# Query and key transposes of the windowed attention put into the score banks 0 and 1 instead of bank 2

## The reference

```python
x = x + _L0_attn_a_ref(_layernorm(x), ...)   # linear attention, 16 heads of 16
x = x + _L0_ffn_ref(_layernorm(x), ...)      # 256 -> 1024 -> 256, ternary weights, relu
x = x + _L0_attn_b_ref(_layernorm(x), ...)   # attention in a window of 64, 16 heads, 4 key heads
x = x + _L0_ffn_ref(_layernorm(x), ...)      # the same feed-forward weights again
```

```python
scores = jnp.einsum('bhqd,bhkd->bhqk', q, k_full) * scale
scores = jnp.where(mask[None, None], scores, jnp.finfo(scores.dtype).min)
att = jax.nn.softmax(scores, axis=-1)
y = jnp.einsum('bhqk,bhkd->bhqd', att, v_full)
...
out = y.transpose(0, 2, 1, 3).reshape(bsz, seqlen, dim) @ Wo.T
```

## Time and profile before

| | before |
|---|---|
| median of 3 runs | 3016.64 us (3013.68 to 3021.11) |
| the profiled execution's own time | 3018.86 us |
| its span | 3017.0 us |
| PE busy | 2801.0 us, 93% |
| DVE busy | 2297.0 us, 76% |
| ACT busy | 1746.8 us, 58% |
| POOL busy | 500.9 us, 17% |
| mean granted clock of TensorE | 0.977 of full speed |

### The profile page before, as it was taken

One profiled execution on the slowest core, in us unless ns is written; L12 is line 12 of the kernel. 1 busy time (PEld: TensorE's weight loads), 2 busy tenths in 40 slices (PEclk: granted clock), 3 DMA queues, 4 the chain that ended last, 5 costly groups with the idle time before them and its releaser, 6 DMA issues.

```text
span 3017.0 us, 75500 instructions
## 1 busy us (share of the span) xinstructions
PE 2801.0 (93%) x25924; PEld 2277.3 (75%) x25924; DVE 2297.0 (76%) x5983; ACT 1746.8 (58%) x3589; POOL 500.9 (17%) x1047
## 2 busy tenths in 40 slices
PE   5789999999999999999999999999999999999976
PEld 4677778877777877777777777777777777777765
DVE  6577787777788777788777788777788777788753
ACT  2356565566655566665566655566656556656553
POOL 4111111111111111111111111101111111111110
PEclk8899999999999999999999999999999999999997
DMA  2000000000000000000000000000000000000000
GB/s 69 8 11 17 17 17 3 14 17 17 17 17 4 13 17 17 17 17 13 4 17 17 17 17 17 3 14 17 17 17 17 3 14 17 17 17 17 4 11 15
DMA packets 42050, 45.04 MB, mean 15 GB/s; under 512 B 2640, under 2 KB 41360, under 8 KB 42000
## 3 DMA queue, kind: packets, MB, share of 16 engines
q1 hardware_dynamic: 42000, 44.40, 4.8%
HBM read 21.32 MB, written 16.78 MB: 13 GB/s over the span
## 4 chain that ended last, share of the span: by engine, by line
PE 68%; DVE 16%; issue 7%; ACT 4%; DMA 3%; DVEq 1%; POOL 0%; SPq 0%; ACTq 0%; POOLq 0%
PE Q L380 18%; PE Y L464 12%; PE HID L440 11%; PE Q L594 4%; PE Q L621 3%; PE HID L388 3%; PE Q L857 3%; DVE a_s L1440 2%; PE Q L644 2%; DMA out<-x 2%; DVE x L1348 2%; ACT a_qz L1170 2%; PE Q L757 2%; PE Q L794 1%; PE Q L873 1%
## 5 line engine op out<-in xcount | busy, mean ns | idle before, releaser
L989 ACT ACTIVATE f_r<-HID,b1c 128x512 f32<-128x512 f32 x512 | 355.1, 694 | 386.0 <-PE HID L440 333.7
L464 PE MATMUL Y<-w2t,f_hh 128*128 128x256 f32 x2048 | 539.4, 296 | 8.5 <-DVE f_hl L1334 8.5
L464 PE MATMUL Y<-w2t,f_hl 128*128 128x256 f32 x2048 | 512.4, 283 | 0.0
L440 PE MATMUL HID<-ff_xh,w1t 128*128 128x512 f32 x1024 | 440.1, 430 | 22.2 <-ACT f_hh L990 16.1
L1334 DVE TENSOR_TENSOR f_hl<-f_r,f_hh 128x512 fp32r<-128x512 f32 x512 | 351.2, 686 | 85.2 <-ACT f_hh L990 80.6
L440 PE MATMUL HID<-ff_xl,w1t 128*128 128x512 f32 x1024 | 410.9, 401 | 0.0
L464 PEld LDWEIGHTS Y<-w2t,f_hh 128*128 128x128 f32 x2048 | 390.1, 190 | 22.0 <-DVE f_hl L1334 14.5
L464 PEld LDWEIGHTS Y<-w2t,f_hl 128*128 128x128 f32 x2048 | 391.1, 191 | 7.4
L990 ACT ACTIVATE f_hh<-HID,b1c 128x512 fp32r<-128x512 f32 x512 | 354.4, 692 | 0.0
L440 PEld LDWEIGHTS HID<-ff_xh,w1t 128*128 128x128 f32 x1024 | 195.9, 191 | 100.8 <-issue 31.7
L1440 DVE TENSOR_TENSOR a_s<-Q,cst 128x512 f32<-128x512 f32 x384 | 246.2, 682 | 27.8 <-PE Q L594 27.7
(11 more groups left out here) (197 smaller groups left out, 7519.1 us busy)
## 6 DMA issues: line engine op xcount, KB each, us to landing
x<-in_x SPq DMA_DIRECT2D x32, 512.0 KB, 4.2
out<-x SPq DMA_DIRECT2D x32, 512.0 KB, 3.1
b_vm<-b_v SPq DMA_DIRECT2D x64, 96.0 KB, 2.1
x<-in_w SPq DMA_DIRECT2D x2, 512.0 KB, 4.3
a_s<-in_w_qkv SPq DMA_DIRECT2D x1, 768.0 KB, 5.0
cst<-in_const SPq DMA_DIRECT2D x1, 645.0 KB, 6.1
ff_xn<-in_w SPq DMA_DIRECT2D x1, 512.0 KB, 7.0
f_r<-in_w SPq DMA_DIRECT2D x1, 512.0 KB, 6.7
```

The lines of the kernel that those rows point to most:

```text
L440: mm = pe.matmul(banks[fb % 2][:], w1t[:, k, fb * P:(fb + 1) * P], src[:, k, :], start=(k == 0 and j == 0), stop=(k == KB - 1 and j == 1))
L464: mm = pe.matmul(Y[t // 2][:, (t % 2) * D:(t % 2 + 1) * D], h[:, fb % 2, t * P:(t + 1) * P], w2t[:, fb, :], start=False, stop=(fb == FB - ...
L989: act.activation(f_r[:, fb % 2, :], banks[fb % 2][:], ACT.Relu, bias=b1c[:, fb:fb + 1]).then_inc(f_rr, 1)
```

## The change

`turn_bank` now names Q[0] for the q stack and Q[1] for the k stack of tiles 1 to 3; the stack of k of tile 0 stays in Q[3] and that of q in Q[2]. ACT's copies read from `turn_bank` too, so they follow. The waits change with the banks: `turn_q(t)` and `turn_k(t)` of tiles 1 to 3 wait for the second and the third exponential of the tile before (which free Q[0] and Q[1]) and no longer for Q[2]. `turn_numer(t)` of tiles 1 to 3 waits for `residual(t - 1)`, as only that of tile 3 did, and that of tile 0 for no bank. The order of all instructions on all engines is the same, and no operation is added or taken away.

```diff
         def turn_bank(t, j):
 
-            return Q[3] if j and t == 0 else Q[2]
+            return (Q[0], Q[1])[j] if t else (Q[2], Q[3])[j]
...
                         if t == 0:
 
                             pe.wait_ge(a_out, a_done * NT)
-                        elif t == 1:
-
-                            pe.wait_ge(b_te, b * 8 + 1)
                         else:
 
-                            pe.wait_ge(b_out, b * NT + t - 1)
+                            pe.wait_ge(b_ex, (b * NT + t - 1) * KVH + 2)
...
                     def turn_k(t):
                         if t:
 
-                            pe.wait_ge(b_te, b * 8 + 2 * t + 1)
+                            pe.wait_ge(b_ex, (b * NT + t - 1) * KVH + 3)
...
                     def turn_numer(t):
                         pe.wait_ge(b_ne, b * NT + t + 1)
-                        if t < NT - 1:
-
-                            pe.wait_ge(b_te, b * 8 + 2 * t + 4)
-                        else:
+                        if t:
 
                             pe.wait_ge(b_out, b * NT + t)
```

## The result

| | before | after |
|---|---|---|
| median | 3015.31 us (3013.68 to 3021.11, 4 runs) | 2984.38 us (2983.65 to 2985.75, 4 runs) |
| ratio to before, 95% interval | | 0.9898 (0.9886 to 0.9910) |
| span of the profiled execution | 3017.0 us | 2983.1 us |
| PE busy | 2801.0 us | 2784.9 us |
| mean granted clock of TensorE | 0.977 | 0.981 |

The change makes the kernel faster by 1.02%, 31 us. Forecast were 19.7 us, and a range that holds the result.

A forecast was written before the change was run, and what follows sets the result against it. The prediction took PE's instruction list to bound the kernel, busy 2801.0 of 3017.0 us. Its terms, 2.0 + 6.2 + 11.5 = 19.7 us, took the median from 3016.64 to 2997 us, with an 8-in-10 range of 2978 to 3009 us.

The forecast's parts named there:

- the full return: Rival: all idle time removed at turn_k(1), turn_q(2) and turn_q(3) comes back; 2977 us, chance 0.13.
- Term A: turn_k(1)'s wait for ACT's copy: gains nothing in ordinary passes, 0.2 us in ten with a clock fall; 2.0 us.
- Term B: turn_q(2)'s wait for residual(0): of 0.33 us idle, 0.2 us a pass comes back before turn_y(1); 6.2 us.
- The 0.14 us at turn_y(1): Time to be had before PE meets the wait for DVE's y: 0.19 us late, where 0.05 was enough.
- the allowance for DVE's own order: Extra 0.06 us at turn_y(1) for DVE's work coming earlier, estimated between nothing and 0.14 us.
- Term C: turn_q(3)'s wait for residual(1): of 0.64 us idle, 0.37 us a pass comes back, limited by ACT's relu; 11.5 us.
- Only term C: Rival: gains at turn_k(1) and turn_q(2) are eaten by DVE, only turn_q(3)'s remains; 3005 us, chance 0.16.
- nothing: Rival: the waits turn up elsewhere, at turn_numer or the next phase 1, so no gain; 3017 us, chance 0.11.
- The clock did not turn against the change: Rival: more clock falls, 0.7 to 1.0 us each, make the kernel slower; 3049 us with 52 more, chance 0.05.

The follow-up runs named there:

- tile 1 alone: Banks and waits of the change for tile 1 only, the other tiles as in the kernel before; 3006.86 us against 3014.81, ratio 0.9972.
- tile 2 alone: Banks and waits of the change for tile 2 only, the other tiles as in the kernel before; 3006.21 us, ratio 0.9963.

## Why the prediction was right, and where it was off

**Direction and mechanism.** Right. turn_q(3), turn_q(2) and turn_k(1) waited on Q[2]; their idle time was removed, 0.23 and about 0.3 us at the last two as worked out, 0.76 us at turn_q(3) where I said 0.64; a second wait stood behind each at the place that was named (numer(2) and next_norm(0), turn_y(1), up(0)). turn_numer did not wait. The median came to 2984.4 where I said 2997: faster, inside the range, and the gain was more than half as large again. That the range held it is due in part to its lower end, which was drawn for the full return and not for the course that I forecast; of the 11 us between forecast and gain about 5 are in the three terms taken together, and 6 in no term at all.

**Term A, the step that failed.** It said that DVE runs without a gap before up(0), so that in the ordinary pass nothing comes back. The timeline marks no idle time there, but DVE's instructions overlap their predecessor by about 0.08 us when nothing holds them, and L1348 started 0.07 us after it. So 0.15 us was to be had, measured by the kernel with tile 1 alone. In passes with a fall I took only the gap that is marked, 0.23 less a little, and the whole 0.48 us came back: DVE's work ahead of it moved too, since it hung on PE as well (its reciprocal L1652 came behind PE's turn_numer(0)). 21 x 0.15 + 10 x 0.48 = 8.0 us where the term said 2.0.

**Term B.** 0.27 us where I said 0.20, 8.4 us for 6.2. The 0.14 us at turn_y(1) was right, and the allowance for DVE's own order too small. That the load of the next input can't come earlier was no limit: with tile 2 alone, where nothing ahead of it moved, the gain was the same. What fixed my 0.06 was a guess between two bounds, and the time is inside them. By the middle values of the ordinary passes y ended 7.10 us after the start of up(0) before, and 6.92 us both after and with tile 2 alone. About half of these 0.18 us is in DVE's own work, which did hang on PE: its reciprocal L1652 came right behind PE's turn_numer(1) in 12 of 19 passes before, and in 4 of 23 after. The other half is the load of the next input, which landed 4.41 us after the start of up(0) before and 4.31 and 4.32 us in these two kernels, though it was issued at the same distance; why it took less stays open.

**Term C.** 0.28 us where I said 0.37, 8.7 us for 11.5. The chain was right (the relu is the last to end), the latency not: 0.144 us, not 0.05. The rows held it already: turn_q(2), with two waits, started at 983.13, 0.15 us after residual(0) ended at 982.98. The idle time itself was read too small, 0.64 for 0.76 us: project(0) to numer(1), taken as a pair without a wait, had one, since numer(1) started 0.13 us after the exponential that it needs in every pass. That changed nothing in the sum, which went by the relu.

**The sum.** 8.0 + 8.4 + 8.7 is 25 us. That is nearer to the 31 measured than my 19.7, and the profiles put the rest outside the ordinary course: the second pass had lost 1.8 us to a late store, which turn_q(2) no longer waits for and which I had counted like all others at 0.2 us, and the first pass and the end are shorter by some us, in part through more time at 2.4 GHz. How much of the end part's 5 us belongs to the change isn't settled: from the start of the last pass but one to the end it was 155 us before and 151 after, and 156, 153 and 149 us in the kernels with one tile moved, with 51, 44, 60, 47 and 31 us of it at the lower clock, in this order; the two repeats of the changed kernel have 151 us as well, with 48 at the lower clock.

**The rivals.** The full return of 39.7 us did not come, as each second wait was real: the passes gained 24.8 us of it, and the 31 us of the whole hold some 6 us from outside the ordinary course. Only term C and nothing are out: each tile alone gives 0.3 to 0.45%. The clock did not turn against the change: ten, nine and seven falls against ten, and PE's idle time went down from 216 to 198 us.

The Trainium skill, in Perfetto Trace Analysis, Optimizing Tensor Performance, Matmuls, says that independent groups should rotate through different PSUM banks so that one's evacuation overlaps the next one's matmuls. The trace agrees in direction, as the idle times behind Q[2] went; what reached the end was set by the next wait.

The Trainium skill, in TensorE: Matmul & The Clock Gate, A second HAM failure mode: psum-queue depth-cycling, reports a kernel whose cycling through banks left PE idle shortly between groups, so that the clock went to and fro. Nothing of this shows here: more banks in turn brought no more falls.

## What to carry to other kernels

When a wait is taken away, the gain is what the next wait in the same list leaves, and that is best found by comparing the spacing of the same pair of groups at a place that waits and one that doesn't. A second engine that shows no idle time may still be waiting: look whether its instruction starts before or after the end of the one ahead, and compare with its usual overlap. One bank more, for the group that shared one with the longest chain, gave all of the gain; check which share is the costly one before giving up two.

## What the runs showed of the hardware

- A PE group that waits for one semaphore started 0.05 to 0.06 us after the end of what it waits for (middle values), most with two waits 0.128 to 0.146 us, even where the other had long been met; with that other wait taken away three such groups came down to 0.053 to 0.056 us. In the traces the slow ones have the late wait on an instruction of PE's sequencer ahead of the weight load. The first turn_q and the first scores of a pass have two waits too, with the late one on the weight load itself, and start at 0.055 us. Their order in the source doesn't tell which wait lands where: the late wait is written first at turn_q(1) and second at turn_q(2) of the kernel before, and both are slow.
- DVE instructions in order mostly start about 0.08 us before the recorded end of the one ahead, if nothing holds them. A wait of up to that length leaves no idle time at all between two records, and the 0.05 to 0.07 us left before L1348 weren't marked in the timeline.
- POOL's chain of six small instructions for the standard deviation took 3.3 us in the pass shown (889.70 to 893.00), where the middle value of that run is 2.6. One of its multiplications, which mostly take 0.20 us, took 0.75 us there, and the next one started 0.83 us after it, where 0.28 us is usual. Such a delay came in other passes too, and the end of the chain then decides when DVE can normalise.
- The fall of the clock near the start of a pass (1.00 to 0.66 in the mean of 5 us, between 2.4 and 1.2 GHz) comes in 7 to 10 of 30 passes of the changed kernel, and in six to 12 over all eleven profiles. By the mean lengths of the 27 whole passes it costs 1.0 us before (90.75 against 89.72) and 0.7 us after (89.74 against 89.01). Part of it is hidden behind turn_q(1)'s wait for the stack: in passes with a fall turn_q(1) comes 0.8 us later in the pass, and PE has no idle time before it, where it has 0.48 us in ordinary ones.
